# Two chained cross-attention layers: orders of steps by place instead of one list per pair of batches, a float32 product for the first batch, layer 1 of the last batch in layer 0's banks

## The reference, cut to what matters

```python
# layer 0
q = emb @ Wq + bq ; k = latent @ Wk + bk ; v = latent @ Wv + bv
w = softmax((q @ k.T) / 16, axis=1)          # over the 512 queries
x = w @ v + emb
x = (x - mean(x)) * rsqrt(var(x) + 1e-6) * gamma + beta
# layer 1, on that x as query
Q = x @ Wq + bq ; K = key @ Wk + bk ; V = key @ Wv + bv
weights = softmax((Q @ K.T) / 16, axis=-1)   # over the 1601 keys
out = x + (weights @ V) @ Wo + bo
```

## Time and profile before

| | us |
|---|---|
| median of 3 runs | 513.74 (513.39 to 514.05) |
| the profiled execution | 513.53 |
| its span in the profile | 511.7 |
| around the span | 1.8 |
| PE busy | 464.3 (91%) |
| DVE busy | 387.2 (76%) |
| ACT busy | 385.2 (75%) |
| POOL busy | 346.2 (68%) |
| mean granted TensorE clock | 0.983 |

### The profile page before, as it was taken

How to read it: one execution, slowest core, us unless ns; L and a number is a source line. 1 busy time by engine, 2 the same in 40 slices (tenths; PEclk the granted TensorE clock), 3 DMA queues, 4 the chain that set the end, 5 groups by cost and what they waited for, 6 DMA issues and landing times.

```text
span 511.7 us, 7981 instructions
## 1 busy us (share of the span) xinstructions
PE 464.3 (91%) x2426; PEld 381.0 (74%) x2426; DVE 387.2 (76%) x920; ACT 385.2 (75%) x798; POOL 346.2 (68%) x319
## 2 busy tenths in 40 slices
PE   8659887999989998999899998999899998799776
PEld 8447555888778886888688885888688886587675
DVE  2355579769986899769977898679976998669744
ACT  3576956998689967997789966987799867872452
POOL 0195966896787948896688857896689768971400
PEclk9989978999999999999999999999999999999989
DMA  8400030000040005000140005000220001000101
GB/s 241 114 0 1 1 106 0 2 2 0 7 141 2 1 1 146 3 0 1 33 115 1 1 2 147 1 0 1 66 83 0 2 3 41 0 1 10 34 0 42
DMA packets 23897, 17.31 MB, mean 34 GB/s; under 512 B 1055, under 2 KB 23854, under 8 KB 23854
## 3 DMA queue, kind: packets, MB, share of 16 engines
...
q10 hardware_dynamic: 4, 0.00, 0.0%
...
## 4 chain that ended last, share of the span: by engine, by line
PE 41%; DVE 36%; ACT 8%; issue 8%; DMA 4%; POOL 2%; SPq 0%; DVEq 0%; POOLq 0%; ACTq 0%
DVE p1T_lo L884 7%; PE ps_s L432 5%; DVE xr L938 5%; PE ps_l L432 5%; PE ps_l L433 5%; PE ps_s L434 5%; PE ps_l L434 5%; PE ps_s L433 5%; DMA x_sb<-in_x_dram 4%; DVE xr L899 4%; PE ps_s L546 4%; DVE s_sb L872 3%; DVE max L951 3%; DVE y_res L978 2%; DVE xhat L930 2%
## 5 line engine op out<-in xcount | busy, mean ns | idle before, releaser
L1069 POOL TENSOR_TENSOR p_lo<-p,p_hi 128x512 fp32r<-128x512 f32 (+1 forms) x104 | 135.2, 1307 | 83.4 <-ACT p_hi L750 83.4
L1062 POOL TENSOR_TENSOR wsum<-wsum,p 128x512 f32<-128x512 f32 (+1 forms) x88 | 115.0, 1307 | 4.6 <-ACT p L742 1.3
L736 ACT ACTIVATE p<-s_sb,min 128x512 f32<-128x512 f32 (+1 forms) x104 | 75.3, 725 | 18.8 <-DVE min L872 16.8
L884 DVE TENSOR_TENSOR p1T_lo<-ps_s,p1T_hi 128x512 fp32r<-128x512 f32 (+1 forms) x104 | 68.0, 681 | 26.7 <-ACT p1T_hi L787 26.5
L787 ACT CAST p1T_hi<-ps_s 128x512 fp32r<-128x512 f32 (+1 forms) x104 | 59.1, 585 | 30.7 <-PE ps_s L546 18.1
L872 DVE CUSTOM_DVE_ANT_0 s_sb<-ps_l,cb 128x512 f32<-128x512 f32 (+1 forms) x104 | 69.8, 683 | 12.5 <-PE ps_l L434 8.9
L742 ACT ACTIVATE p<-p,r 128x512 f32<-128x512 f32 (+1 forms) x104 | 73.1, 719 | 4.4 <-DVE r L879 3.9
L951 DVE TENSOR_REDUCE max<-ps_s 128x1 f32<-128x804 f32 x60 | 59.1, 994 | 15.7 <-PE ps_s L434 13.3
L750 ACT CAST p_hi<-p 128x512 fp32r<-128x512 f32 (+1 forms) x104 | 63.4, 618 | 1.3 <-PE ps_l L434 0.7
L546 PE MATMUL ps_s<-ident,p 128*128 128x128 f32 (+1 forms) x416 | 58.7, 279 | 5.0 <-ACT p L779 5.0
L546 PEld LDWEIGHTS ps_s<-ident,p 128*128 128x128 f32 (+1 forms) x416 | 50.4, 145 | 14.6 <-ACT p L779 7.3
(11 more groups left out here) (163 smaller groups left out, 1063.8 us busy)
## 6 DMA issues: line engine op xcount, KB each, us to landing
ctx_sb<-in_ctx_dram SPq DMA_DIRECT2D x24, 256.0 KB, 4.9
...
out_dram<-y_res SPq DMA_DIRECT2D x16, 256.0 KB, 2.2
p<-in_L_xattn_Wq_dram SPq DMA_DIRECT2D x2, 256.0 KB, 3.7
...
p<-in_L_xattn_Wo_dram SPq DMA_DIRECT2D x1, 256.0 KB, 4.7
```

What stands on the lines that cost most here:

```text
L736: nc.scalar.activation(p0[0:m, ring0(i), :], s0_sb[0:m, (a.par + i) % 2, :], ACT.Exp, bias=min0[0:m, i:i + 1], scale=-1.0, accum_out=sum0[ ...
L884: nc.vector.tensor_tensor(p1T_lo[0:m, i % RING, :], ps_turn[i % 3][0:m, :], p1T_hi[0:m, i % RING, :].bitcast(F32), ALU.subtract).then_inc( ...
L1062: nc.gpsimd.tensor_tensor(total, total, p0[0:m, ring0(i), :], ALU.add).then_inc(wsum_done, 1)
L1069: nc.gpsimd.tensor_tensor(p0_lo[0:m, h, :], p0[0:m, ring0(i), :], p0_hi[0:m, h, :].bitcast(F32), ALU.subtract).then_inc(p0_lo_done, 1)
```

## The change

Every step of every engine gets a number, its place, per batch; batch n's places are shifted by n times 100000, and the engine runs all steps of all batches sorted by place. There are three tables for each engine: STEADY, FIRST (batch 0) and LAST (batch 7), each with an order of its own. `pre1` is no block any more but steps `prepare` 0 to 5 with places of their own in FIRST. Steps that did four row blocks at once are split to one step a row block (`bias_x0`, `normalised`, `bias_row1`, `residual1` into `gamma_y` and `beta_y`), with semaphore counts to match. Waits for the next batch's use of a bank are for the last reader of that bank. The ring `p0` has 5 places for all tiles (before: 4, and one for the last tile), and its next writer waits for `p0_low` instead of the product. Batch 0 has no `p0_high` and no `p0_low`: its `weigh0` is one float32 matmul on the unrounded operands. Layer 1 of batch 7 uses the four banks of `ps_l0` alone, and its `p1` rows lie in the room of x, context and `p0`.

```diff
+STEADY, FIRST, LAST = range(3)
+SLOT = 100000
+IN_FLOAT = (0,)
...
+def program(places, batches):
+    steps = []
+    for n in range(batches):
+        own = {**places[STEADY], **(places[FIRST] if n == 0 else places[LAST] if n == batches - 1 else {})}
+        steps += [(SLOT * n + at, n, name, i) for (name, i), at in own.items() if at is not None]
+    return [(n, name, i) for _, n, name, i in sorted(steps)]
...
-    R0 = 4
+    R0 = 5
...
+        def l1_bank(b, k):
+            return (ps_l0 if last(b) else ps_s1)[:, k * BANK:(k + 1) * BANK]
+        def s1_banks(b):
+            return (ps_l0 if last(b) else ps_s1)[:].rearrange("p (k m) -> p k m", m=BANK)
...
+                if a.n in IN_FLOAT:
+                    pe.wait_ge(norm0_done, MT * a.n + i + 1)
+                    mm = nc.tensor.matmul(ps_acc0[:], ctx_sb[a.par][0:m, i, :], p0[0:m, ring0(a, i), :], **ends)
...
+                if last(b) and c == 0:
+                    pe.wait_ge(xr_done, 2 * B)
+                elif last(b):
+                    pe.wait_ge(at0_lo_done, B)
+                elif not first(b) and c == 0:
+                    pe.wait_ge(p1T_lo_done, MT * b.n)
+                elif not first(b):
+                    pe.wait_ge(at1_done, b.n)
...
-                    if not first(b):
-                        pe.wait_ge(o_done, 2 * b.n)
                     pe.wait_ge(qw1_lo_done, b.n + 1)
-                before = t - 2 if last(b) else t - 1
-                if before >= 0 and k in (0, len(chunks) - 1):
-                    pe.wait_ge(exp1_done, 2 * (TB * b.n + before) + (1 if k == 0 else 2))
+                if t == 0 and k in (1, 2) and not first(b) and not last(b):
+                    pe.wait_ge(o_done, 2 * (b.n - 1) + k)
+                if t and k in (0, len(chunks) - 1):
+                    pe.wait_ge(exp1_done, 2 * (TB * b.n + t - 1) + (1 if k == 0 else 2))
...
+                k = MT * a.n + i - R0
+                if k >= 0:
+                    act.wait_ge(wsum_done, k + 1)
+                if k >= 0 and k // MT in split:
+                    act.wait_ge(p0_lo_done, halves(batch(k // MT), k % MT) + 1)
+                elif k >= 0:
+                    act.wait_ge(pv0_ps, k + 1)
...
+            def bias_row1(b, t):
+                dve.wait_ge(row1_made, MADE)
+                dve.wait_ge(xhat_done, TB * b.n + t + 1)
...
+            def prepare(_, i):
+                if i == 0:
+                    turn_weights(1, s1_bank(0), s1_bank(1))
+                    pe.wait_ge(wv_loaded, 16 * 3)
```

More of the change, by code:

```diff
@@ L601, in pre0 @@
                 turn_vectors(0, ps_acc0)
[L602 to L603 removed]
+                turn_x(batch(0), 0)
+                turn_x(batch(0), 1, s1_bank(3))
                 keep_warm(WARM[1])
@@ L684, in _ @@
             steps = {f.__name__: f for f in (
-                turn_x, project_q0, project_bias0, turn_ctx, scores0, weigh0, sum_rows0, predict, turn_y, project_q1, scores1, turn_p1, weigh1, project_out)}
-            def body(a, b, c, done=()):
-                for step, (name, who, i) in enumerate(TENSOR_ORDER):
-                    bt = {"a": a, "b": b, "c": c}[who]
-                    if bt and (name, i) not in done:
-                        if name in MISC:
-                            misc_read(step, a, b, c, done)
-                        steps[name](bt, i)
-            run(body, (pre0, pre1), pe)
+                turn_x, project_q0, project_bias0, turn_ctx, scores0, weigh0, sum_rows0, predict, turn_y, project_q1, scores1,
+                turn_p1, weigh1, project_out, prepare)}
+            pre0()
+            held = None
+            for n, name, i in after_start(TENSOR):
+                if name in MISC:
+                    if held:
+                        misc_read(*held)
+                    held = name, batch(n), i
+                steps[name](batch(n), i)
         @blk.scalar
@@ L838, in _ @@
+            steps = {f.__name__: f for f in (
+                x_turned, q0_high, bias0, ctx_high, ctx_split, exp0, norm0, p0_high, weighed0, y_turned, q1_high, exp1,
+                p1_turned, weighed1, prepare)}
+            pre0()
+            for n, name, i in after_start(SCALAR):
+                steps[name](batch(n), i)
         @blk.vector
@@ L1044, in _ @@
+            steps = {f.__name__: f for f in (
+                ctxT_low, xT_low, at0_low, bias_x0, q0_low, max0, recip0, residual0, moments0, normalised, bias_row1, q1_low,
+                rowmax1, bias1_of, recip1, p1_low, finish, prepare)}
+            pre0()
+            for n, name, i in after_start(VECTOR):
+                steps[name](batch(n), i)
         @blk.gpsimd
@@ L1096, in pre0 @@
                                         pattern=[[-1, P]], channel_multiplier=1).then_inc(ident_done, 1)
[L1098 to L1110 removed]
+            steps = {f.__name__: f for f in (ctx_low, sum_weights, p0_low, rsqrt_var, gamma_y, beta_y)}
+            pre0()
+            for n, name, i in after_start(GPSIMD):
+                steps[name](batch(n), i)
 _INS = ["x", "ctx_512"] + [f"L0_xattn_{n}" for n in ("Wq", "bq", "Wk", "bk", "Wv", "bv", "gamma", "beta")] + [
```

559 lines of the change are left out of this document (295 added, 264 removed), and 208 rows, old and new, of tables (GPSIMD, GPSIMD_ORDER, SCALAR, SCALAR_ORDER).

## The result

The kernel after takes 530.0 us (median of 4 runs, 529.1 to 533.1) against 513.9 for the kernel before beside it: ratio 1.028, 95% interval 1.023 to 1.033. The forecast was 498, faster; it is 3% slower. The profiled execution took 530.54 us, its span is 528.7, 17.0 longer than before.

A forecast was written before the change was run, and what follows sets the result against it. PE was taken to bound the middle but not the ends. From 513.53, start -13.8, steady spacings -9.0 and -1.4, last spacing -1.0 and end +9.8 gave 498.1, stated as 498, range 489 to 509.

The forecast's parts named there:

- Start: Span up to batch 0's q1_low, 85.84 before: forecast at 72.0, 13.8 less, bounds 68.4 to 79.3.
- The ledger: PE's work from 16.7 to batch 0's last weigh0, summed to 38.5, so ending at 55.2.
- Steady spacings: Six spacings between q1_low starts: 9.0 less from shorter PE waits (bounds 0 to 13.5), 1.4 less from moved work.
- The expected gains: Per steady spacing, 0.8 of PE's 1.36 wait for q1_low and the 0.68 wait for x go.
- The ceiling: In a steady spacing of 56.65 PE is busy 54.40, so reordering alone can take at most 2.25.
- Last spacing: The seventh spacing between q1_low starts, 48.96 before: net 1.0 less, bounds +2 and -3.
- End: Span after batch 7's q1_low, 37.53 before: 9.8 more, bounds +6 and +17.
- The banks' term: Batch 7's scores on one set of banks take 22.4 instead of 13.80, 8.6 more.
- The 1.2 for `bias_row1`: Three bias_row1 on DVE between batch 7's first and second row block's maxima cost 1.2 more.
- the clock, a rival: PE falls to half rate in the gaps of batch 7's scores: 6.6 more, 504.7; chance 0.12.
- The slower one: Queue inversion: ACT's exp0 5 waits for POOL's sum_weights 1, delaying project_q1 seven times; 519 at 3.0 a spacing; chance 0.08.
- a measurable difference: For the whole kernel, a measurement can tell 0.2%, 1.0 us, from no change.

The follow-up runs named there:

- a_split: Kernel after with batch 0's float product undone, back to p0_high, p0_low and three matmuls per tile; ratio 1.0501 to the kernel before.
- b_wsum: Kernel before with POOL's sum_weights 1 and 2 of the next batch moved behind rsqrt_var 1; ratio 1.0318 to the kernel before.
- a_free: Kernel after with two last-batch bank sets, bias_row1, recip1 and sum_weights 1 moved, POOL kept off DVE's three groups; ratio 0.9556 to the kernel before.
- b_free: Kernel before with one more wait: POOL's p0_low 2 waits for the batch before's four bias_row1; 494.1 us, ratio 0.9535.
- a_recip: Kernel after with recip1 moved behind p1_low 5 on DVE; ratio 1.0199 to the kernel before.
- a_warm2: Kernel after with 12 small filler products behind each tile of the last batch's scores; ratio 1.0121 to the kernel before.
- b_banks: Kernel before with the last batch's four score tiles on one set of banks; ratio 1.0229 to the kernel before.
- a_both: Kernel after with sum_weights 1 and 2 ahead of rsqrt_var 0 and two bank sets for the last batch; ratio 0.9914 to the kernel before.
- a_best: a_both plus recip1 behind p1_low 5 and the last batch's three further bias_row1 ahead of q1_low; ratio 0.9765 to the kernel before.

## Why the prediction was wrong, point by point

- **Start.** -13.8 forecast, -11.3 measured, inside 68.4 to 79.3. The ledger held: the wait for Wo came (2.3), the block's wait of 5 went, and the last `weigh0` of batch 0 ended at 58.7, where 55.2 and 3.6 of stalls and slow matmuls had been added up to 58.8. The chain behind it took 15.9 for the 13.2 of the estimate; that is the miss. How much of the gain the float product carries is open: `a_split` shows only that this order needs it.
- **Steady spacings: the step that failed.** It said "The counts of work are the same" and then priced DVE's dense stretch with durations of the earlier trace rows, as if they belonged to the instructions. They belonged to what POOL did beside them: `bias_row1` at 1.17 was 0.48 of work. And the sentence that "the splitting into row blocks, the ring of five and the waits per bank cost nothing by themselves" left POOL's reordering unpriced; `b_wsum` shows that two POOL steps in another place cost 18.9. The lower bound, 0 gained, was argued from PE's waits moving; a loss was not excluded by any reason, and should have been in it. What came instead of a gain was +13.2, because `normalised`, 0.41 each before, took 1.28 beside POOL's moved additions, and PE waits for it. The expected gains did come (in the six spacings no wait for x and one of 0.7 for `q1_low`) and were overlaid by 2.1 to 2.4 a spacing for xhat in five, and by 0.5 to 1.1 for max and 0.8 for xr in four. In two spacings the clock came on top: PE is busy 56.41 and 56.05 there for 54.80, at 0.97, after the wait for xhat. The longest, 61.70, also has a `bias_row1` of 4.08 and behind it a wait of 1.3 of PE for `q0_low`, as in `a_free`.
- **The ceiling.** "PE busy 54.40: 2.25 are left, and nothing that only reorders can take more" is false. `b_free` only makes POOL wait, and spacings are 53.8, less than the busy time of 54.40 for the same work. Busy time of PE is thus no floor; what made it longer is not shown. DVE's "29.35 busy of 30.76" was none either: 2.7 of it were `bias_row1` waiting for POOL (4 x (1.17 - 0.48), an estimate).
- **Last spacing.** +2.6 for -1.0, half a microsecond outside its bounds; 1.25 of it is `recip1`'s place (`a_recip`).
- **End.** +12.6 for +9.8. The banks' term, a stretch of 22.4, held: 22.6 in `a_warm2`, where the clock is held up. The 1.2 for `bias_row1` did not show: the cycles at full rate are 5.5 with it (`a_warm2`) and without it (`b_banks`). With two sets of banks the same rows cost up to 2.7, `a_both` to `a_best`, where the clock rises too. What was missing is the clock, a rival with 0.12 and 6.6 us, 2.2 in each of three blocks; it came, at 5, in two cycles (6.8 and 7.4 long for 5.5) and in the first transposes behind them (0.61 in 504.67 to 512).
- **The rivals.** The slower one sat at the right place (the additions behind `rsqrt_var` 1) with the wrong mechanism: it saw ACT's ring waiting for POOL, and ACT's list has but one wait for wsum, of 1.1. What was late was DVE, beside POOL and not behind it.
- **What can be told.** The 1.0 us that the forecast called a measurable difference was too fine: the kernel after's runs lie 4.0 apart, and the same kernel before took 513.9 beside it and 518 beside the experiments.

What stays open: why the fourth row of `bias_row1` in `a_free` lasted over three POOL instructions and not one; how much of the start is the float product; and whether after's start and `b_free`'s spacings can be had together (about 7 us), for which the fourth row would have to be guarded too.
